# Ninth harmonic's products in 64-row matmuls, and feature rows doubled by ScalarE, in the fourth edge stage of a graph network

## The chip, the core and the metric

One core of one Trainium2 chip runs the whole network. The metric is device time in microseconds, the median of repeated runs.

## The reference, cut to what matters

Four graph layers follow each other on 3,125 nodes with 64 features and 53,125 edges sorted by destination. The change touches the fourth, an equivariant attention. With `x` the normalised features, per edge:

```
def tensor_product(x_e, sh, w, C):          # x_e [E,64], sh [E,9], C [64,9,128]
    acc = sh[:, 0:1] * (x_e @ C[:, 0, :])
    for s in range(1, 9):
        acc = acc + sh[:, s:s + 1] * (x_e @ C[:, s, :])
    return acc * w
k = tensor_product(x[edge_dst], edge_sh, wk, Cqk)     # keys,   128 columns
v = tensor_product(x[edge_dst], edge_sh, wv, Cv)      # values, 128 columns
attn = einsum('ehd,ehd->eh', q[edge_src], k)          # 8 heads of 16
alpha = segment_softmax(attn, edge_src)
upd = segment_sum(v * alpha, edge_src)                # then W_out, W_self, batch norm
```

(The reference hands `src, dst` over as this layer's `edge_dst, edge_src`, so the kernel gathers features by `src_i` and queries by `dst_i`.) The nine harmonics are a contraction over 9 x 64 = 576 rows: four and a half times the 128 rows of TensorE.

## The kernel before

Edges are padded to 416 tiles of 128, four tiles (GT = 4) to a **group**, so the stage has 104 groups. Weights of keys and values (`WKV`) were written to memory by the third stage. Each engine has its own instruction list; they meet at semaphores.

- **GpSimd (POOL)** gathers, per group, four tiles of feature rows from `XX` (L1780) into a ring `ga` of four groups, and four tiles of query rows from `QW` (L1770). `XX` has 128 columns: each node's 64 features, twice. The features are written twice by VectorE (L2035) and ScalarE (L1884) and stored before the stage (L1825).
- **SyncE (SP)** loads the harmonics, repeated over 64 partitions each: `shb` partitions 0 to 63 hold harmonics 0, 2, 4, 6, 8 (L1801), partitions 64 to 127 hold 1, 3, 5, 7 and zeros in the fifth place (L1802, L2039). It also loads `wkv` (L1794).
- **TensorE (PE)** in step s: `transposes(s)` puts the four doubled feature tiles, transposed, into bank 0 (L1926); `products(s-1, t)` for t = 0 to 3 are each five matmuls of 128 rows and 256 columns (L1935), which the profile shows as ten records, since an fp32 matmul has two passes; between them stand the sums over edges of group s-8 in two halves (L1916, L1917), and pieces of the softmax.
- **VectorE (DVE)** in step s: `harmonics(s)` multiplies bank 0 by `shb` into `z` (L2052), `keys_and_values(s-2)`, `add_sums(s-8)` in two halves (L2091, L2096), `values(s-7)` (L2079), and pieces of the softmax.
- **ScalarE (ACT)** in step s: one-hot matrices for group s-5 (L1845, L1849), and `weights(s-7)`: `ob` (L1856) and three copies into `D` (L1860), the latter behind a wait for `xb`, the split of the exponents that VectorE makes with its casts (L727 to L730).

The softmax works on four groups at once. Its pieces lie in two of every four steps: `soft_1` in steps with k % 4 == 2, `soft_2` in those with k % 4 == 3. In the second, VectorE ends the step with the exponents and their split (`split_steps`), then `values`. PE's list for a step begins

```
if lag(i, k, 0):
    transposes(i, k)
if p1:
    softmax_pe_0(pe, S3, q, 8, am3[:, b])
for t in range(GT):
    if kv:
        products(*kv, t)
    if old and t == 0:
        sums(*old, 0)
```

so whatever holds the transposes of group s holds the products of group s-1 too.

Of the kernel before, what the change touches and what calls it, by code (L numbers as in the profile page):

```python
# [27 lines left out]
ACT = mybir.ActivationFunctionType  # L28
AX = mybir.AxisListType

N = 3125
D = 64
E = 53125
PN = 125
# [58 lines left out]
def build(nc, A, out):  # L93
    with ExitStack() as ctx:
# [22 lines left out]
        def dram(name, shape, dt=F32):  # L117
            return nc.dram_tensor(name, shape, dt, kind="Internal").ap()
# [1463 lines left out]
        with nc.Block() as block:  # L1582
# [108 lines left out]
        w_self = sb("w_self", [D, D])  # L1691
        gcol = sb("gcol", [D, 1])
        bcol = sb("bcol", [D, 1])
        XX = dram("XX", [N, 2 * D])
        QW = dram("QW", [N, F])
        n3_l, n3_p, n3_dve, n3_var, n3_std, n3_t, n3_tc, n3_q, n3_qc, n3_ox, n3_oq, n3_h, n3_x = [sem("n3_" + x) for x in
            ("l", "p", "dve", "var", "std", "t", "tc", "q", "qc", "ox", "oq", "h", "x")]
        NL3 = 9
        R3 = rounds(NJ, 4)
        HALVES = [(slice(0, 12), 3), (slice(12, NJ), len(R3))]  # L1700
        PARTS = [(0, 3), (3, 5), (5, 7)]
# [3 lines left out]
        e3_g = [sem(f"e3_g{k}") for k in range(UG)]  # L1705
        QR = 4
        NODE3 = len(R3) * 5 + 2
        e3_zero = sem("e3_zero")
        e3_gq = [sem(f"e3_gq{k}") for k in range(UG)]
        e3_e = [sem(f"e3_e{k}") for k in range(2)]  # L1710
        e3_n = [sem(f"e3_n{k}") for k in range(2)]
# [15 lines left out]
        nodes = z[0:PN].rearrange("p a z e -> p (a z e)")  # L1727
        XC = nodes[:, 0:NJ * D].rearrange("p (j f) -> p j f", j=NJ)
        yn = nodes[:, NJ * D:2 * NJ * D].rearrange("p (j f) -> p j f", j=NJ)
        twice = nodes[:, NJ * D:3 * NJ * D].rearrange("p (j a f) -> p j a f", j=NJ, a=2)  # L1730
        D3 = tmp("D3", [128, 2, GT, 128], BF16)
        ob = tmp("ob3", [128, 2, GT * W], BF16)
        am3 = tmp("am3", [128, 2, 128])
# [29 lines left out]
        with nc.Block() as block:  # L1763
            @block.gpsimd
            def _(pool):
                def queries(g):
                    if g >= QR:
                        pool.wait_ge(e3_ev, (g - QR + 1) * 2)
                    for t in range(GT):
                        pool.indirect_dma_start(qg[:, (g % QR) * GT + t, :], None, QW, bass.IndirectOffsetOnAxis(  # L1770
                            ap=dst_i[:, g * GT + t:g * GT + t + 1], axis=0)).then_inc(e3_gq[g % UG], 16)

                pool.memset(ckv[D:128, NZ - 1, :], 0.0).then_inc(n3_p, 1)
                groups = NT // GT
                pool.wait_ge(n3_ox, len(HALVES) * 16)
                for g in range(groups):
                    if g >= GR:
                        pool.wait_ge(e3_X, g - GR + 1)
                    for t in range(GT):
                        pool.indirect_dma_start(ga[:, (g % GR) * GT + t, :], None, XX, bass.IndirectOffsetOnAxis(  # L1780
                            ap=src_i[:, g * GT + t:g * GT + t + 1], axis=0)).then_inc(e3_g[g % UG], 16)
                    if g == 1:
                        pool.wait_ge(n3_dve, NODE3)
                        pool.wait_ge(n3_oq, len(PARTS) * 16)
                    if g:
                        queries(g - 1)
                queries(groups - 1)

            @block.sync
            def _(sp):  # L1790
                def weights_load(i, k):
                    g = i * UG + k
                    wait(sp, e3_ev, (g - 1) * 2)
                    sp.dma_start(wkv[:, k % 2].rearrange("p t f -> p (t f)"),  # L1794
                                 WKV[:, bass.ds(g * GT * 2 * F, GT * 2 * F)]).then_inc(e3_n[k % 2], 16)

                def harmonics_load(i, k):
                    g = i * UG + k
                    cols = bass.ds(g * GT * W, GT * W)
                    wait(sp, e3_z, g - 1)  # L1800
                    sp.dma_start(shb[0:D, k % 2], A["ea9"][0:NS:2, cols].partition_broadcast(D)).then_inc(e3_e[k % 2], 16)  # L1801
                    sp.dma_start(shb[D:128, k % 2, 0:NZ - 1], A["ea9"][1:NS:2, cols].partition_broadcast(D)).then_inc(e3_e[k % 2], 16)  # L1802

                def body(i, k):
                    if lag(i, k, 0) and i * UG + k >= 2:
                        harmonics_load(i, k)
                    if lag(i, k, 2) and i * UG + k >= 4:
                        weights_load(*lag(i, k, 2))
                L = lambda o, i: sp.dma_start(o, i).then_inc(n3_l, 16)
                L(wq[:], A["L3_gnn_Wq"])  # L1810
                L(w_out[:], A["L3_gnn_W_out"])
                L(w_self[:], A["L3_gnn_W_self"])
                with nc.allow_non_contiguous_dma(reason="biases as columns"):
                    L(gcol[:], A["L3_gnn_gamma"].rearrange("a f -> f a"))
                    L(bcol[:], A["L3_gnn_beta"].rearrange("a f -> f a"))
                for m, w in ((ckv[:, :, 0:F], "Cqk"), (ckv[:, :, F:2 * F], "Cv")):
                    L(m[0:D, :, :], A["L3_gnn_" + w][:, 0:NS:2, :])
                    L(m[D:128, 0:NZ - 1, :], A["L3_gnn_" + w][:, 1:NS:2, :])
                for k in range(2):
                    harmonics_load(0, k)  # L1820
                for k in range(2):
                    weights_load(0, k)
                for h, (J, _) in enumerate(HALVES):
                    sp.wait_ge(n3_x, h + 1)
                    sp.dma_start(XX.rearrange("(p j) f -> p j f", p=PN)[:, J, :], twice[:, J].rearrange("p j a f -> p j (a f)")).then_inc(n3_ox, 16)  # L1825
                for part in PARTS:
                    sp.wait_ge(n3_qc, part[1])
                    sp.dma_start(QW.rearrange("(p j) f -> p j f", p=PN)[:, J_of(part), :], tab[:, J_of(part), :]).then_inc(n3_oq, 16)
                sp.wait_ge(e3_pad, 1)
                each_step(sp, body)  # L1830

            @block.scalar
            def _(act):
# [17 lines left out]
                def weights(i, k):  # L1851
# [7 lines left out]
                    for part in range(3):  # L1859
                        act.activation(D3[:, k % 2, :, part * 8:(part + 1) * 8],  # L1860
                                       exb[:, s, part, :].rearrange("p (x t) -> p t x", x=8)[:, kk * GT:(kk + 1) * GT, :],
                                       ACT.Copy).then_inc(e3_Mx, 1)

                def body(i, k):
                    p1, p2 = soft_1(i, k), soft_2(i, k)
                    if p1:
                        softmax_act_1(act, S3, p1[0] * 2 + p1[1], 8)
                    if p2:
                        softmax_act_3(act, S3, p2[0] * 2 + p2[1], 8)
                    if lag(i, k, 5):  # L1870
                        one_hots(*lag(i, k, 5))
                    if p2:
                        softmax_act_4(act, S3, p2[0] * 2 + p2[1], p2[1], 8, 1)
                        softmax_act_5(act, S3, p2[0] * 2 + p2[1], p2[1], fac_cols, 2)
                    if lag(i, k, SUMS - 1):
                        weights(*lag(i, k, SUMS - 1))
# [2 lines left out]
                    act.wait_ge(m2_x, r + 1)  # L1879
                    act.activation(yn[:, J, :], XC[:, J, :], ACT.Square).then_inc(m2_q, 1)  # L1880
                ln_std_step(act, n3_var, n3_std, 1)
                for h, (J, _) in enumerate(HALVES):
                    act.wait_ge(n3_h, h + 1)
                    act.activation(twice[:, J, 1, :], twice[:, J, 0, :], ACT.Copy).then_inc(n3_x, 1)  # L1884
                for r, (j0, n) in enumerate(R3):
                    act.wait_ge(n3_t, r + 1)
                    act.activation(HT[0:D, j0 * PN:(j0 + n) * PN], bank[r % 2][0:D, 0:n * PN], ACT.Copy).then_inc(n3_tc, 1)
# [7 lines left out]
            def _(pe):  # L1895
# [24 lines left out]

                def transposes(i, k):
                    g = i * UG + k
                    pe.wait_ge(e3_g[k], i * 64 + 64)
                    wait(pe, e3_z, g)
                    for t in range(GT):
                        last = pe.transpose(bank[0][:, t * 128:(t + 1) * 128], ga[:, (k % GR) * GT + t, :], ident[:])  # L1926
                    last.then_inc(e3_X, 1)

                def products(i, k, t):
                    g = i * UG + k  # L1930
                    if t == 0:
                        pe.wait_ge(e3_z, g + 1)
                        wait(pe, e3_ev, (g - 1) * 2)
                    for j in range(NZ):
                        last = pe.matmul(kv_of(k)[:, t, :], z[:, k % 2, j, t * 128:(t + 1) * 128], ckv[:, j, :],  # L1935
                                         start=(j == 0), stop=(j == NZ - 1))
                    if t == GT - 1:
                        last.then_inc(e3_V, 1)

# [29 lines left out]
                def node_transposes(r):  # L1969
# [2 lines left out]
                    if r >= 2:  # L1972
                        pe.wait_ge(n3_tc, r - 1)
                    for j in range(n):
                        last = pe.transpose(bank[r % 2][0:D, j * PN:(j + 1) * PN], twice[:, j0 + j, 0, :], ident[0:PN, 0:PN])
                    last.then_inc(n3_t, 1)

                def node_queries(r):
# [20 lines left out]
                        node_queries(r - 1)  # L1999
                node_queries(len(R3) - 1)  # L2000
                pe.wait_ge(n3_qc, len(R3))
                pe.wait_ge(n3_p, 1)
                pe.sem_inc(e3_S, SPARE)
                each_step(pe, body)

# [1 line left out]
            def _(dve):  # L2007
# [24 lines left out]
                dve.wait_ge(n3_std, 1)  # L2032
                c.link(dve.reciprocal(st[:, 5, :], st[:, 4, :]))
                for J, _ in HALVES:
                    dve.scalar_tensor_tensor(twice[:, J, 0, :], XC[:, J, :], 0.0, st[:, 5, J].unsqueeze(2).to_broadcast([PN, J.stop - J.start, D]),  # L2035
                                             ALU.max, ALU.mult).then_inc(n3_h, 1)
                c.mark(dve.tensor_scalar(dst_i[:], dst_i[:], 0, None, ALU.max))
                assert c.n == NODE3
                dve.memset(shb[D:128, :, NZ - 1, :], 0.0).then_inc(e3_pad, 1)  # L2039
                dve.memset(acc[:, 0:2, :], 0.0).then_inc(e3_zero, 1)  # L2040
                dve.memset(D3[:], 0.0).then_inc(e3_i, 1)
                dve.memset(crow[:], -BIG).then_inc(e3_i, 1)
# [4 lines left out]
                def harmonics(i, k):  # L2047
                    g = i * UG + k
                    dve.wait_ge(e3_X, g + 1)
                    dve.wait_ge(e3_e[k % 2], i * (UG // 2 * 32) + (k // 2 + 1) * 32)  # L2050
                    wait(dve, e3_V, g - 1)
                    dve.tensor_tensor(z[:, k % 2], bank[0][:].unsqueeze(1).to_broadcast([128, NZ, GT * W]), shb[:, k % 2],  # L2052
                                      ALU.mult).then_inc(e3_z, 1)
# [268 lines left out]
```

## Time and profile before

| | |
|---|---|
| median of 3 runs | 3109.23 us (3104.41 to 3112.86) |
| profiled execution: its time, its span | 3103.95 us, 3102.2 us |
| mean granted TensorE clock | 0.871 |
| first and last `harmonics` of the fourth stage | 1892.0 and 3001.3 us |
| busy in the span | PE 79%, DVE 71%, POOL 66%, ACT 28% |

A row of windows gives the stretch and its length, then busy us and number of instructions for PE, PE's weight loads, DVE, ACT and POOL, then the granted clock, the share of the DMA engines and GB/s. The profile is one execution. Times in a timeline are us from the start of the span. A granted clock of 1.00 is 2.4 GHz and 0.50 is 1.2 GHz. Busy time of PE counts overlapping records once; the end of a matmul is modelled, so the distance between starts says more than a duration.

### The profile page before, as it was taken

The numbers are of one execution on the slowest core, as the hardware profiler recorded it, in microseconds if no ns is written. First come the engines' busy times: TensorE is split into PE (matmuls) and PEld (weight loads), VectorE is DVE, ScalarE is ACT, GpSimd is POOL, SyncE is SP. The second block draws the span as 40 slices with busy tenths as digits, with TensorE's granted clock in tenths as the row PEclk, the third lists the DMA queues.
The fourth block names the chain that finished last, engine by engine and source line by source line (L and its number), as shares of the span: only waits on it lengthen the run. The fifth ranks groups of instructions, "written<-read, shape, count | busy, mean of one in ns | idle before, by whom it ended". The sixth has DMA issues, their size and how long they took to land. (4 is left out here: it accounts for less than half of the span.)

```text
span 3102.2 us, 51526 instructions
## 1 busy us (share of the span) xinstructions
PE 2460.4 (79%) x14042; PEld 2123.0 (68%) x14042; DVE 2187.5 (71%) x5057; ACT 868.7 (28%) x2421; POOL 2033.7 (66%) x2116
## 2 busy tenths in 40 slices
PE   5877777525766667477787767999999999999997
PEld 4777777424666666355565556888888888888884
DVE  4655555526888888555555564788888888888885
ACT  1111111136666664111111111223222233222233
POOL 4777777457777771177777745777777776767730
PEclk9777777657888888599989987999999999999996
DMA  3443333133333330044545456988889888898850
GB/s 85 94 93 87 86 86 85 31 65 65 59 60 61 61 56 7 29 153 153 162 153 161 153 150 162 219 213 206 206 206 213 208 206 203 209 211 208 202 137 11
DMA packets 333728, 404.37 MB, mean 130 GB/s; under 512 B 171120, under 2 KB 202974, under 8 KB 333538
## 3 DMA queue, kind: packets, MB, share of 16 engines
q1 hardware_dynamic: 252002, 251.19, 34.8%
q0 software_dynamic: 66560, 96.41, 14.0%
q10 hardware_dynamic: 14976, 54.53, 5.1%
q8 instruction: 84, 1.38, 0.2%
q14 instruction: 106, 0.87, 0.1%
HBM read 339.81 MB, written 62.07 MB: 130 GB/s over the span
## 5 line engine op out<-in xcount | busy, mean ns | idle before, releaser
L1935 PE MATMUL psum<-ckv,z 128*128 128x256 f32 x4160 | 968.2, 383 | 0.0
L1935 PEld LDWEIGHTS psum<-ckv,z 128*128 128x128 f32 x4160 | 766.9, 191 | 98.0
L1770 POOL DMA_INDIRECT acc<-QW,dst_i x416 | 400.2, 962 | 183.6 <-issue 111.2
L234 POOL DMA_INDIRECT ga<-TA,src_i x416 | 409.5, 984 | 160.8 <-issue 126.5
L1780 POOL DMA_INDIRECT ga<-XX,src_i x416 | 400.5, 963 | 163.8 <-issue 122.3
L1027 POOL DMA_INDIRECT ga<-T,src_i x416 | 402.5, 968 | 152.7 <-issue 125.9
L234 POOL DMA_INDIRECT ga<-T,src_i x416 | 399.2, 960 | 149.3 <-issue 124.3
L2052 DVE TENSOR_TENSOR z<-psum,shb 128x2560 f32<-128x2560 f32 x104 | 293.2, 2820 | 67.8 <-PE psum L1926 67.5
L1121 PE MATMUL psum<-HT,wy 128*128 128x128 f32 x1664 | 260.2, 320 | 69.0 <-DVE wy L1394 68.8
L445 PE MATMUL psum<-wre,re 128*128 128x68 f32 x832 | 208.6, 342 | 132.7 <-DVE oneT L290 80.9
L1121 PEld LDWEIGHTS psum<-HT,wy 128*128 128x128 f32 x1664 | 238.3, 228 | 87.1 <-DVE wy L1394 80.9
L445 PEld LDWEIGHTS psum<-wre,re 128*128 128x128 f32 x832 | 168.0, 250 | 154.8 <-issue 149.0
L1668 DVE TENSOR_TENSOR acc<-acc,psum 64x128 f32 x416 | 118.5, 285 | 158.3 <-PE psum L1623 114.0
L1623 PE MATMUL psum<-one,ga 128*128 128x128 f32 x832 | 129.1, 303 | 121.1 <-DMA ga<-T,src_i 109.4
L1623 PEld LDWEIGHTS psum<-one,ga 128*128 128x128 f32 x832 | 113.0, 208 | 152.7 <-issue 136.8
L1607 PEld LDWEIGHTS psum<-w2kv,hid 128*128 128x128 f32 x832 | 163.2, 196 | 72.0 <-issue 54.0
L446 PE MATMUL psum<-win,oneT 128*128 128x64 f32 x832 | 203.2, 335 | 0.0
L1607 PE MATMUL psum<-w2kv,hid 128*128 128x256 f32 x832 | 201.4, 386 | 0.0
L2096 DVE TENSOR_TENSOR acc<-acc,psum 128x256 f32 x416 | 175.5, 422 | 35.4 <-PE psum L1917 22.1
L1636 ACT ACTIVATE hid<-psum,b1kv 128x512 f32<-128x512 f32 x104 | 71.5, 687 | 455.1 <-PE psum L1615 455.1
L1202 DVE TENSOR_TENSOR acc<-acc,psum 128x256 f32 x416 | 173.4, 417 | 26.2 <-DVE acc L1202 8.6
L407 ACT ACTIVATE msg<-pre 128x256 f32<-128x256 f32 x104 | 43.5, 418 | 475.3 <-DVE pre L500 431.4
(366 smaller groups left out, 4198.2 us busy)
## 6 DMA issues: line engine op xcount, KB each, us to landing
shb<-in_ea SPq DMA_DIRECT2D x104, 640.0 KB
WKV<-wkvo ACTq DMA_DIRECT2D x104, 512.0 KB
shb<-in_ea SPq DMA_DIRECT2D x104, 512.0 KB
wkv<-WKV SPq DMA_DIRECT2D x104, 512.0 KB
dl<-DL SPq DMA_DIRECT2D x208, 128.0 KB
win<-TB SPq DMA_DIRECT2D x416, 32.0 KB
ga<-T,src_i POOLq DMA_INDIRECT x832
ef<-in_ea SPq DMA_DIRECT2D x104, 128.0 KB
```

The source lines that it names most:

```text
L234: pool.indirect_dma_start(o, None, table, bass.IndirectOffsetOnAxis(ap=src_i[:, g * GT + t:g * GT + t + 1], axis=0)).then_inc(s_g[k], 16)
L445: pe.matmul(P[:, o:o + D + 4], re[:, k % ER, t * W:(t + 1) * W], wre[:], start=True, stop=False)
L446: last = pe.matmul(P[:, o:o + D], oneT[:, k % 2, t * 128:(t + 1) * 128], win[:, k * GT + t, 0:D], start=False, stop=True)
L1027: pool.indirect_dma_start(ga[:, ring(g) + t, :], None, T1, bass.IndirectOffsetOnAxis(ap=src_i[:, g * GT + t:g * GT + t + 1], axis=0)).then ...
L1121: last = pe.matmul(sums_of(n)[:, a * 128:(a + 1) * 128], wy[:, g % YR, t, 2 * a:2 * a + 2, :].rearrange("p h f -> p (h f)"), one[:, g % OR ...
L1607: last = pe.matmul(kvp(k)[:, t * 256:(t + 1) * 256], hid[:, k % 2, t * 128:(t + 1) * 128], w2kv[:], start=True, stop=True)
L1623: last = pe.matmul(bank[k % 2][:, t * 128:(t + 1) * 128], ga[:, pair:pair + 2, :].rearrange("p a f -> p (a f)"), one[:, k * GT + t, :], st ...
L1770: pool.indirect_dma_start(qg[:, (g % QR) * GT + t, :], None, QW, bass.IndirectOffsetOnAxis(ap=dst_i[:, g * GT + t:g * GT + t + 1], axis=0) ...
L1780: pool.indirect_dma_start(ga[:, (g % GR) * GT + t, :], None, XX, bass.IndirectOffsetOnAxis(ap=src_i[:, g * GT + t:g * GT + t + 1], axis=0) ...
L1935: last = pe.matmul(kv_of(k)[:, t, :], z[:, k % 2, j, t * 128:(t + 1) * 128], ckv[:, j, :], start=(j == 0), stop=(j == NZ - 1))
L2052: dve.tensor_tensor(z[:, k % 2], bank[0][:].unsqueeze(1).to_broadcast([128, NZ, GT * W]), shb[:, k % 2], ALU.mult).then_inc(e3_z, 1)
L2096: dve.tensor_tensor(a, a, sums_of(half)[:, (t % 2) * 256:(t % 2 + 1) * 256].rearrange("p (r n) -> p r n", r=2), ALU.add).then_inc(e3_acc, 1)
```

## The change

- The ninth harmonic's fifth chunk, before a 128-row matmul per tile with 64 rows of zeros, becomes a 64-row matmul per tile. Tiles 0 and 1 use partitions 0 to 63, tiles 2 and 3 partitions 64 to 127, so `shb` and `ckv` hold the ninth harmonic and its weights there also. All four are issued ahead of tile 0's other matmuls, in the order 0, 2, 1, 3: the halves alternate, and so do the two banks of PSUM they write.
- `XX` holds each node once (64 columns). The gather fills columns 0 to 63 of `ga`; ScalarE copies them to columns 64 to 127 (`second_halves`), first in its step, after a wait for the gather. TensorE's transposes wait for that copy. The double features before the stage and their copy by ScalarE go.
- A third harmonics load per group for SP (64 partitions x 256 columns), two more weight loads.

```diff
-        XX = dram("XX", [N, 2 * D])
+        XX = dram("XX", [N, D])
...
-                pool.memset(ckv[D:128, NZ - 1, :], 0.0).then_inc(n3_p, 1)
...
-                        pool.indirect_dma_start(ga[:, (g % GR) * GT + t, :], None, XX, bass.IndirectOffsetOnAxis(
+                        pool.indirect_dma_start(ga[:, (g % GR) * GT + t, 0:D], None, XX, bass.IndirectOffsetOnAxis(
...
+                    late = bass.ds(g * GT * W + 2 * W, 2 * W)
+                    sp.dma_start(shb[D:128, k % 2, NZ - 1:NZ, 2 * W:], A["ea9"][NS - 1:NS, late].partition_broadcast(D)).then_inc(e3_e[k % 2], 16)
...
+                    L(m[D:128, NZ - 1:NZ, :], A["L3_gnn_" + w][:, NS - 1:NS, :])
...
-                    sp.wait_ge(n3_x, h + 1)
-                    sp.dma_start(XX.rearrange("(p j) f -> p j f", p=PN)[:, J, :], twice[:, J].rearrange("p j a f -> p j (a f)")).then_inc(n3_ox, 16)
+                    sp.wait_ge(n3_h, h + 1)
+                    sp.dma_start(XX.rearrange("(p j) f -> p j f", p=PN)[:, J, :], H[:, J, :]).then_inc(n3_ox, 16)
...
+                def second_halves(i, k):
+                    act.wait_ge(e3_g[k], i * 64 + 64)
+                    rows = ga[:, (k % GR) * GT:(k % GR + 1) * GT, :]
+                    act.activation(rows[:, :, D:F], rows[:, :, 0:D], ACT.Copy).then_inc(e3_two, 1)
+
                 def body(i, k):
                     p1, p2 = soft_1(i, k), soft_2(i, k)
+                    if lag(i, k, 0):
+                        second_halves(i, k)
...
-                for h, (J, _) in enumerate(HALVES):
-                    act.wait_ge(n3_h, h + 1)
-                    act.activation(twice[:, J, 1, :], twice[:, J, 0, :], ACT.Copy).then_inc(n3_x, 1)
...
-                    pe.wait_ge(e3_g[k], i * 64 + 64)
+                    pe.wait_ge(e3_two, g + 1)
...
                     if t == 0:
                         pe.wait_ge(e3_z, g + 1)
                         wait(pe, e3_ev, (g - 1) * 2)
-                    for j in range(NZ):
+                        for u in (0, 2, 1, 3):
+                            half = slice(0, D) if u < 2 else slice(D, 128)
+                            pe.matmul(kv_of(k)[:, u, :], z[half, k % 2, NZ - 1, u * 128:(u + 1) * 128], ckv[half, NZ - 1, :],
+                                      start=(u % 2 == 0), stop=False, skip_group_check=True)
+                    for j in range(NZ - 1):
                         last = pe.matmul(kv_of(k)[:, t, :], z[:, k % 2, j, t * 128:(t + 1) * 128], ckv[:, j, :],
-                                         start=(j == 0), stop=(j == NZ - 1))
+                                         start=False, stop=(j == NZ - 2), skip_group_check=True)
...
-                dve.memset(shb[D:128, :, NZ - 1, :], 0.0).then_inc(e3_pad, 1)
+                dve.memset(shb[D:128, :, NZ - 1, 0:2 * W], 0.0).then_inc(e3_pad, 1)
```

The rest of the diff renames `twice` to `H` where it is read and written, and adjusts counts of semaphores.

## Rows read from the trace of the kernel before

**Rows 1.** One window of 900 us in the fourth stage
```profile
2000.00:2900.00 900.00, 894.39 (x4846) 785.86 (x4845) 787.23 (x1605) 262.30 (x830) 652.23 (x679) 1.00 0.88 208
```
**Rows 2.** Groups of instructions by line, 2000 to 2900 us
```profile
L1935 PE MATMUL psum<-ckv,z 128*128 128x256 f32 x3329 | 773.4, 382 | 0.0
L1780 POOL DMA_INDIRECT ga<-XX,src_i x340 | 327.2, 962 | 103.7 <-issue 100.0 <-PE psum L1926 3.7
```
**Rows 3.** Waits, 2000 to 3000 us: total, times, longest
```profile
DVE acc L2096 <- PE psum L1917: 15.8, 23, 0.7
...
DVE z L2052 <- PE psum L1926: 11.4, 23, 0.6
```
**Rows 4.** Timeline, all engines: end of a soft_2 step and the step behind
```profile
2405.19 0.52 PE L701 MATMUL psum<-fdiag,sel 128*128 128x16 f32 x4
...
2405.55 0.63 PE L1926 MATMUL psum<-ident,ga 128*128 128x128 f32 x4
...
2407.34 0.23 DVE L730 CAST exb<-exf 128x128 bf16<-128x128 f32 x1
2407.66 0.56 ACT L1860 ACTIVATE D<-exb 128x32 bf16<-128x32 bf16 x3 [1.20 <-DVEq L732]
...
2408.12 1.26 ACT L1845 ACTIVATE one<-iota_row,dloc 128x128 f32<-128x128 f32 x4
2408.39 2.82 DVE L2052 TENSOR_TENSOR z<-psum,shb 128x2560 f32<-128x2560 f32 x1
...
2416.44 0.60 PE L1926 MATMUL psum<-ident,ga 128*128 128x128 f32 x4
...
2417.14 2.82 DVE L2052 TENSOR_TENSOR z<-psum,shb 128x2560 f32<-128x2560 f32 x1
```
**Rows 5.** Timeline of the next two steps
```profile
2424.89 0.42 DVE L2096 TENSOR_TENSOR acc<-acc,psum 128x256 f32 x1 [0.72 <-PE psum L1917]
...
2426.84 0.60 PE L1926 MATMUL psum<-ident,ga 128*128 128x128 f32 x4
...
2427.48 2.83 DVE L2052 TENSOR_TENSOR z<-psum,shb 128x2560 f32<-128x2560 f32 x1 [0.47 <-PE psum L1926]
...
2438.61 2.82 DVE L2052 TENSOR_TENSOR z<-psum,shb 128x2560 f32<-128x2560 f32 x1
```
**Rows 6.** Timeline of VectorE where the cycle of four closes
```profile
2451.59 2.82 DVE L2052 TENSOR_TENSOR z<-psum,shb 128x2560 f32<-128x2560 f32 x1
```
**Rows 7.** Groups by line and form, ScalarE, whole span
```profile
L407 ACT ACTIVATE msg<-pre 128x256 f32<-128x256 f32 x104 | 43.5, 418 | 475.3 <-DVE pre L500 431.4 <-PE psum L432 25.7 <-issue 18.2
```
**Rows 8.** Timeline near the stage's start
```profile
1911.68 1.12 PE L1926 MATMUL psum<-ident,ga 128*128 128x128 f32 x4 [4.66 <-DMA ga<-XX,src_i]
...
1912.59 11.33 PE L1935 MATMUL psum<-ckv,z 128*128 128x256 f32 x40
...
1924.19 8.80 PE L1935 MATMUL psum<-ckv,z 128*128 128x256 f32 x40
```
**Rows 9.** Windows in the same stretch, columns as in rows 1
```profile
1913.00:1917.00 4.00, 4.00 (x11) 3.17 (x10) 3.90 (x4) 0.00 (x0) 3.13 (x3) 0.50 0.17 49
1917.00:1919.00 2.00, 2.00 (x9) 1.68 (x8) 1.25 (x3) 0.00 (x0) 1.39 (x3) 0.82 0.77 212
```
**Rows 10.** Windows in the third stage, around pauses of PE
```profile
1704.50:1707.50 3.00, 0.41 (x3) 0.07 (x1) 1.91 (x3) 0.00 (x0) 2.10 (x3) 1.00 0.65 202
...
1744.50:1747.50 3.00, 0.44 (x3) 0.04 (x2) 1.83 (x3) 0.00 (x0) 2.11 (x3) 0.92 0.69 219
1747.50:1750.50 3.00, 3.00 (x10) 2.48 (x11) 0.55 (x2) 0.00 (x0) 2.39 (x3) 0.51 0.15 33
```
**Rows 11.** Timeline ahead of the stage
```profile
1864.52 1.25 SPq L1825 DMA_DIRECT2D XX<-z  x2
...
1878.65 0.95 POOL L1780 DMA_INDIRECT ga<-XX,src_i  x1 [37.25 <-DMA XX<-z]
```
**Rows 12.** Timeline of the stage's first gathers of queries
```profile
1894.51 0.94 POOL L1770 DMA_INDIRECT acc<-QW,dst_i  x1 [6.14 <-DMA QW<-vw]
```

More of the change, by code:

```diff
@@ L1697, in build @@
             ("l", "p", "dve", "var", "std", "t", "tc", "q", "qc", "ox", "oq", "h", "x")]
-        NL3 = 9
+        NL3 = 11
         R3 = rounds(NJ, 4)
@@ L1707, in build @@
         NODE3 = len(R3) * 5 + 2
-        e3_zero = sem("e3_zero")
+        e3_zero, e3_two = sem("e3_zero"), sem("e3_two")
         e3_gq = [sem(f"e3_gq{k}") for k in range(UG)]
@@ L1729, in build @@
         yn = nodes[:, NJ * D:2 * NJ * D].rearrange("p (j f) -> p j f", j=NJ)
-        twice = nodes[:, NJ * D:3 * NJ * D].rearrange("p (j a f) -> p j a f", j=NJ, a=2)
         D3 = tmp("D3", [128, 2, GT, 128], BF16)
@@ L1974, in node_transposes @@
                     for j in range(n):
-                        last = pe.transpose(bank[r % 2][0:D, j * PN:(j + 1) * PN], twice[:, j0 + j, 0, :], ident[0:PN, 0:PN])
+                        last = pe.transpose(bank[r % 2][0:D, j * PN:(j + 1) * PN], H[:, j0 + j, :], ident[0:PN, 0:PN])
                     last.then_inc(n3_t, 1)
@@ L2001, in _ @@
                 pe.wait_ge(n3_qc, len(R3))
-                pe.wait_ge(n3_p, 1)
                 pe.sem_inc(e3_S, SPARE)
@@ L2034, in _ @@
                 for J, _ in HALVES:
-                    dve.scalar_tensor_tensor(twice[:, J, 0, :], XC[:, J, :], 0.0, st[:, 5, J].unsqueeze(2).to_broadcast([PN, J.stop - J.start, D]),
+                    dve.scalar_tensor_tensor(H[:, J, :], XC[:, J, :], 0.0, st[:, 5, J].unsqueeze(2).to_broadcast([PN, J.stop - J.start, D]),
                                              ALU.max, ALU.mult).then_inc(n3_h, 1)
@@ L2049, in harmonics @@
                     dve.wait_ge(e3_X, g + 1)
-                    dve.wait_ge(e3_e[k % 2], i * (UG // 2 * 32) + (k // 2 + 1) * 32)
+                    dve.wait_ge(e3_e[k % 2], i * (UG // 2 * 48) + (k // 2 + 1) * 48)
                     wait(dve, e3_V, g - 1)
```

## The prediction, as put on record before the result

> **What bounds the kernel now.** I read the busy shares by window first, to find the stage's limit; then the groups by line, for what one group of edges costs each engine; then the waits, for who is really held; and then the timeline of four steps, because the softmax comes once in four groups and a mean over them hides where the slack lies.
>
> From 2000 to 2900 us PE is busy 894.39 of 900 us at clock 1.00, DVE 787 [rows 1]. The products alone are 3329 records, 83.2 groups of 40, and 773 us of the 894 [rows 1, 2]. So a group takes 900 / 83.2 = 10.81 us. POOL needs 0.962 us for a gather and 0.30 behind it (100.0 / 340 [rows 2]); I take the query gathers as the same. Eight of them are 10.1 us a group: POOL is 0.7 us from being the bound.
>
> DVE's 87% looks like slack, but the waits say otherwise: over 1000 us it waits for PE only 15.8 + 11.4 = 27 us [rows 3], 0.29 us a group. The rest of its idle time is its own waits from one instruction to the next. A PE of no cost would leave about 10.5 us a group. The four steps show the same. From one z to the next the distances are 8.75, 10.34, 11.13 and 12.98 us, together 43.20 [rows 4 to 6]. Only the second holds waits for PE, 0.72 and 0.47 us [rows 5]. PE's list for a plain step is 10.40 us (2416.44 to 2426.84 [rows 4, 5]).
>
> **The change, part by part.**
>
> *Products.* At 1924.19 forty passes take 8.80 us from the start of the first to the end of the last [rows 8]; one record is 0.382 us [rows 2]. So the pitch is (8.80 - 0.38) / 39 = 0.216 us, and the tail of a pass 0.17 us. Per group eight passes of 128 rows (1.73 us) go and eight of 64 rows come. No row shows 64-row matmuls on alternating halves, so I bound them. Perfectly paired they take four slots, 0.86 us: a saving of 0.87. Not overlapping at all, with the array run empty where the shape changes (twice 0.17), they take 2.07: a loss of 0.34. Between: passes start in order and each matmul has two on the same half (A A B B C C D D), so only the second of one and the first of the next overlap: five slots, 1.08 us, and one to two tails. I take 1.33 us, a saving of 0.40 us a group, so a plain PE step is 10.00 us.
>
> The tail of 0.17 us is what an emptied array would cost by the rows [rows 2, 8]. The Trainium skill's page "TensorEngine Tiling (Array Packing)", section "Key Properties", speaks against this change: a change of tiling mode drains TensorE, and there are two per group. By that rule the block takes 1.08 + 0.34 = 1.42 us and the step 10.09; with no drain 1.08 and 9.75. The cycle worked out below would lose 2.14 or 1.46 us by these, instead of 1.96.
>
> *The copy on ScalarE.* 128 x 256 elements take 0.418 us [rows 7]; ScalarE is busy 262 of 900 us [rows 1], so its time costs nothing. Its place does. It stands first in step s+1 of ScalarE's list, behind `weights(s-7)` of step s, and in a soft_2 step those end with the `D` copies, which wait for DVE's last cast. That cast ends at 2407.34 + 0.23 = 2407.57; the `D` copies start at 2407.66 and the next ScalarE instruction could start at 2408.12 [rows 4]. The copy then ends near 2408.54. Before, PE began these transposes at 2405.55 [rows 4], right behind the softmax's small matmuls of 2405.19. In the changed kernel PE waits about 3 us there, and behind the waiting transposes in its list stand the products of the group before, whose z has long been ready, and the sums, for which DVE waits.
>
> Where does it go? DVE's z comes at: last cast 2407.57, + 0.97 (copy done), + 0.06 release and 0.2 weight load, + 0.60 transposes, + 0.04 = 1.87 us behind the cast, against 0.82 before (2408.39 [rows 4]). So the fourth distance grows by 1.05 to 14.03. Then PE has had no lead left: transposes directly ahead of z, and a whole PE step between two transposes. So the first distance is no longer DVE's 8.75 but PE's 10.00, and the second too is 10.00 (before 10.34; DVE's own is 9.15). The third stays DVE's 11.13. Sum 10.00 + 10.00 + 11.13 + 14.03 = 45.16 us, 1.96 more than 43.20. There are 26 softmax blocks, and 24 of their soft_2 steps have transposes behind them: 24 x 1.96 = **+47 us**.
>
> *The clock.* PE's small matmuls wait for DVE, so they stay near 2405.19 + 0.52 in that frame (at most 0.8 us earlier), and the transposes move to about 2408.8. PE is idle 3 to 4 us, with little work just ahead. In this trace a pause of 4.66 us was followed by clock 0.50 up to about 1917.6, the transposes taking 1.12 instead of 0.60 and 40 passes 11.33 instead of 8.80 [rows 8, 9]: 3.0 us of PE's time. In the third stage pauses near 2.6 us come about every 10 us; the clock mostly stays at 1.00, as at 1704.5, but in about one of four falls to 0.50, as at 1744.5, for some 3 us of work [rows 10], which costs 1.5 us. The new pause lies between, nearer to the long one. I take a fall in 21 of 24 and 2.2 us each: 21 x 2.2 = **+46 us**. It falls on the two steps where PE has become the bound, so it isn't hidden. The page "TensorE: Matmul & The Clock Gate" of the Trainium skill, section "Loop structure matters more than you think", warns of the same: matmuls behind a long wait run cold. The rows agree at 4.66 us and are mixed at 2.6.
>
> *Gather and loads.* The feature gather moves half the bytes, the third harmonics load adds 64 KB against 128 KB less, on DMA engines busy 0.88 [rows 1]; SP issues one more DMA of about 0.6 us a group and has room. The loads for a group are asked for two steps ahead, about 18 us. Cost 0; if the cover were gone, a DMA a fraction of a microsecond late per group. POOL's 10.1 us stay below the new 11.3.
>
> *Ahead of the stage.* `XX` has half the bytes and is stored without ScalarE's copy. POOL now starts at 1878.65, 13 us behind the two stores' issue of 1864.52 [rows 11]; half of that may go. But its second round waits for the query table until 1894.51 [rows 12], so most is only an earlier wait. I take -2 us, bounds -6 and +1. The first seven groups run at POOL's rate; nothing comes of PE's saving there. The tail behind the last z doesn't change.
>
> Sum: 47 + 46 - 2 = +91 us. The profiled execution took 3103.95 us (span 3102.2), which would become 3195; the runs' median is 5.3 us above it, so 3109.23 + 91 = **3200 us**.
>
> **The rivals.**
>
> *The stall without the clock.* If PE's pause leaves the clock at 1.00, as most pauses of 2.6 us do [rows 10], only 47 - 2 remain: 3154. With perfect pairs the PE step is 9.54 and the cycle 44.24 (+1.04): 25 us, and -6 ahead: 3128, the low bound.
>
> *Pairs that don't overlap.* The PE step is 10.73, the cycle 10.73 + 10.73 + 11.13 + 14.03 = 46.62 (+3.42): 82 + 46 - 2 = 126, so 3235. With 3.0 us for each of 24 falls it is 82 + 72: 3263, the high bound. For it speaks that two passes of a matmul share a half, against it that the halves and banks alternate.
>
> *Faster: the copy is hidden everywhere.* If ScalarE had the doubled rows ready before PE came, the 0.72 + 0.47 us in the second distance would vanish and the other three stay: 42.01 us, -1.19 x 24 = -29, with -2 ahead 3078. It decides by one thing: whether the copy ends ahead of 2405.55 in the frame of [rows 4]. It is queued behind the `D` copies of 2407.66. Only if PE's lead in that step were not needed at all would the result come near this.
>
> *No change.* The stall costs less than worked out (PE's lead partly kept) and the clock stays, so that about 1 us a cycle of loss meets the saving of rival three.
>
> **How the numbers follow.** Within 0.3%, 9 us, no difference can be told. Chances: forecast with stall and clock (3165 to 3230) 0.58; stall without clock (3128 to 3165) 0.18; no overlap (3225 to 3263) 0.12; hidden copy 0.07; no change 0.05. Slower 0.88, same 0.05, faster 0.07. The range is 3138 to 3240: it leaves out the faster and unchanged cases (0.12) and the ends of the second and third (about 0.07).
>
> **What the changed profile would show.** In every fourth step the wait of PE's transposes for ScalarE's copy, 3 to 4 us, directly behind `D`; z 1.9 us behind the last cast; clock 0.50 for 3 to 6 us in 21 of 24 such places; distances near 10 + 10 + 11.1 + 14, with 2 us more on the first. The eight 64-row passes within about 1.3 us. PE's busy share falls from 99% though DVE's falls too. The prediction is wrong if PE does not wait for the copy there, if DVE's z in the step behind comes at 8.75 again, if the clock reads 1.00 throughout, or if the 64-row block takes over 1.8 us.

## The result, and the profile after

The changed kernel takes 3204.45 us (median of 4 runs, 3201.53 to 3207.88) against 3106.82 us before: a ratio of 1.032, with a 95% interval from 1.0302 to 1.0337. The prediction was 3200 us, in a range from 3138 to 3240. The profiled execution has a span of 3199.8 us, 97.6 more than before.

One window of the fourth stage, columns as in [rows 1]:

```profile
2000.00:2900.00 900.00, 827.56 (x4391) 682.33 (x4390) 718.58 (x1449) 261.32 (x831) 585.10 (x614) 0.93 0.78 183
```

Every engine is less busy than in [rows 1], and the clock is 0.93 in the mean. No engine has become a bound. Waits have come, and the waits from 2000 to 3000 us (total, times, longest) name them:

```profile
PEld psum L1931 <- ACT ga L1868: 78.0, 21, 4.2
...
DVE acc L2104 <- PE psum L1922: 74.8, 59, 2.6
...
DVE z L2060 <- PE psum L1931: 38.5, 63, 1.3
```

The first row is new: 21 times in 1000 us PE waits for the copy. The other two are those of [rows 3], 27 us then and 113 us now: VectorE waits for a TensorE that has come late. The timeline at the end of one soft_2 step answers to [rows 4]:

```profile
2440.69 0.59 PE L701 MATMUL psum<-fdiag,sel 128*128 128x16 f32 x4
...
2443.61 0.23 DVE L730 CAST exb<-exf 128x128 bf16<-128x128 f32 x1
2443.92 0.56 ACT L1861 ACTIVATE D<-exb 128x32 bf16<-128x32 bf16 x3 [1.89 <-DVEq L732]
...
2444.39 0.40 ACT L1868 ACTIVATE ga<-ga 128x256 f32<-128x256 f32 x1
...
2444.84 1.12 PE L1931 MATMUL psum<-ident,ga 128*128 128x128 f32 x4 [3.56 <-ACT ga L1868]
...
2445.99 2.83 DVE L2060 TENSOR_TENSOR z<-psum,shb 128x2560 f32<-128x2560 f32 x1 [1.25 <-PE psum L1931]
```

This is the chain that the prediction named: last cast, `D` copies, the new copy, transposes, z. The transposes take 1.12 us instead of 0.63, so z comes 2.15 us behind the cast (2443.84 to 2445.99), where 1.87 was worked out at full clock and 0.82 was seen before. Windows of the same place show the clock:

```profile
2443.00:2444.50 1.50, 0.00 (x0) 0.00 (x0) 1.20 (x4) 0.58 (x4) 1.08 (x2) 0.62 1.09 391
2444.50:2446.00 1.50, 1.16 (x6) 0.84 (x6) 0.25 (x2) 1.47 (x6) 1.00 (x2) 0.50 0.16 34
2446.00:2449.00 3.00, 3.00 (x11) 1.99 (x12) 3.00 (x2) 1.99 (x6) 1.82 (x2) 0.50 0.16 31
...
2450.50:2452.00 1.50, 1.50 (x12) 1.37 (x11) 1.24 (x4) 0.00 (x0) 0.94 (x1) 1.00 0.77 208
```

The clock falls inside the pause and is back at 1.00 some 5 us behind the restart. It fell at each of the 22 pauses from 2000 to 3050 us (3.55 to 4.07 us long); the mean time at half clock behind a restart was about 5.2 us. The one pause of the stage at which it did not fall lasted 2.48 us.

The 64-row block, by the weight loads of PE in one plain step:

```profile
2504.87 0.57 PEld L1931 LDWEIGHTS psum<-ident,ga 128*128 128x128 f32 x4
2505.61 0.73 PEld L1941 LDWEIGHTS psum<-ckv,z 64*128 64x128 f32 x8 [0.17 <-issue]
2506.68 1.59 PEld L1944 LDWEIGHTS psum<-ckv,z 128*128 128x128 f32 x8 [0.33 <-issue]
```

From the first 64-row load to the next 128-row load are 1.07 us, and the engine's loads stand idle ahead of each change of shape (0.17 and 0.33 us). In the kernel before no load waits at this place. I read this as the array running empty twice; how much time it costs is measured in p11_in_place below. A plain step of PE is 9.94 us (transposes at 2409.66 and 2419.60), where 10.00 was forecast.

Read from the starts of z in the timelines, medians over the stage, in us (the first distance follows the soft_2 step; the last column is the mean cycle of four steps from group 8 to group 96):

| kernel | 1st | 2nd | 3rd | 4th | mean cycle |
|---|---|---|---|---|---|
| before | 8.75 | 10.33 | 11.13 | 12.98 | 43.40 |
| changed | 12.00 | 10.11 | 11.29 | 14.30 | 47.67 |

### The profile page after: what moved, and what is told of

The parts are those of the page before. It is cut to its first block and busy times, and to the rows that moved or that the text cites. A ratio compares the mean times of both kernels' runs of the same rounds, so it can differ in the third digit from the quotient of the medians.

```text
span 3199.8 us, 51733 instructions
## 1 busy us (share of the span) xinstructions
PE 2485.4 (78%) x14042; PEld 2086.3 (65%) x14042; DVE 2194.6 (69%) x5057; ACT 900.0 (28%) x2523; POOL 2022.1 (63%) x2115
## 5 line engine op out<-in xcount | busy, mean ns | idle before, releaser
L1944 PE MATMUL psum<-ckv,z 128*128 128x256 f32 x3328 | 822.0, 395 | 0.0
L1944 PEld LDWEIGHTS psum<-ckv,z 128*128 128x128 f32 x3328 | 625.2, 196 | 125.2 <-issue 42.8
L1769 POOL DMA_INDIRECT acc<-QW,dst_i x416 | 393.6, 946 | 298.8 <-DVE vw L2075 190.0
L1846 ACT ACTIVATE one<-iota_row,dloc 128x128 f32<-128x128 f32 x416 | 131.8, 388 | 185.4 <-PE psum L1922 185.4
```

## The experiments

All medians below are set against the kernel before on the same chip (3103.6 to 3106.3 us).

**p1_products.** The change's products without its copy: the kernel before with

```diff
+  third harmonics load, ninth harmonic's weights also on partitions 64 to 127
+  for u in (0, 2, 1, 3): 64-row matmuls ahead of tile 0's others
   (XX and the gathers stay 128 columns wide, no second_halves)
```

> The 64-row products alone: features gathered double as before, no copy on ScalarE. Theory (the copy's place is the whole loss, the new products are a gain): PE's plain step 9.94 us as in the changed kernel, VectorE becomes the bound, the four distances of z are about 8.75, 9.15, 11.1, 13.0 (sum 42.0 against 43.2), no fall of the clock after the softmax step, time 3078 (24 x -1.2 us), ratio near 0.991. Rival (the change of matmul shape costs as much as it saves): distances as before, 3100 to 3112. Rival (the 64-row block itself is a loss): over 3120.

3098.67 us (3087 to 3127 in ten runs), ratio 0.9991 (0.9964 to 1.0018): no difference to the kernel before can be told. The medians of the distances are near the theory's: 8.75, 9.34, 11.35, 12.92. But the mean cycle is 43.34, because some second and third steps are longer, up to 13.4 us, and the time is not 3078. Waits and one window say why:

```profile
DVE z L2057 <- DMA shb<-in_ea: 16.8, 17, 2.6
```

```profile
2000.00:2900.00 900.00, 870.23 (x4878) 721.35 (x4876) 788.68 (x1610) 262.16 (x830) 654.95 (x679) 1.00 1.00 214
```

The DMA engines are busy all the time, and z waits for the harmonics. I read this as a third load together with double gathers being more than they carry at this pace; p8_no_third_load takes the load away, and p7_early_mid further down has the load with single gathers (DMA share 0.94, 3084.75 us). So the halved gather is not there for nothing, a thing that neither of my theories had.

**p8_no_third_load.** The same without the third load. The kernel leaves out the ninth harmonic's part of tiles 2 and 3, which it multiplies by zeros, so it serves only to measure time:

```diff
-  sp.dma_start(shb[D:128, k % 2, NZ - 1:NZ, 2 * W:], ...)
+  dve.memset(shb[D:128, :, NZ - 1, :], 0.0)     # whole row zero, as before
```

> The kernel with the 64-row products alone and double gathers, without the third harmonics load: the ninth harmonic of tiles 2 and 3 is left out (multiplied by zeros). Theory (that kernel's VectorE waited for harmonics on DMA engines busy all the time): DMA share down from 1.00 to about 0.95, no wait of z for shb, 3080 to 3090 against 3099. Rival (the waits come from something else): 3099.

3084.22 us, ratio 0.9936 (0.9920 to 0.9951). DMA share 0.92, no wait of z for `shb`, mean cycle 42.39:

```profile
2000.00:2900.00 900.00, 879.59 (x4953) 733.03 (x4952) 803.62 (x1638) 265.26 (x840) 674.87 (x693) 1.00 0.92 213
```

So the third load on top of the double gathers costs p1_products some 15 us.

**p2_copy.** The change's copy without its products:

```diff
-  for u in (0, 2, 1, 3): ...   # 64-row matmuls
-  for j in range(NZ - 1): ...
+  for j in range(NZ): ...      # five 128-row matmuls per tile, two loads, as before
```

> The copy on ScalarE alone, products all in 128-row matmuls as before. Theory: the same wait of the transposes in every fourth step and the same fall of the clock, with a PE step of 10.4 us in place of 9.94, so the two steps bound by PE cost 0.9 us more in a cycle of four than in the changed kernel: 3204 + 24 x 0.9 = 3226. Rival (the stall comes from the products' new form or from loads): near 3110.

3196.62 us, ratio 1.0295 (1.0274 to 1.0316). That the stall is the copy's is shown: the kernel loses 90 us with no 64-row matmul in it. The size was missed by 30 us, and the other way: it is faster than the whole change. Its distances are 12.08, 10.40, 11.13, 13.85. The second is PE's longer step, as expected; the first should have been near 13. PE, which comes later to the transposes, pauses less:

```profile
2443.30 0.93 PE L1929 MATMUL psum<-ident,ga 128*128 128x128 f32 x4 [2.87 <-ACT ga L1866]
```

2.87 us, not 3.56. The clock falls at 20 of 23 such pauses and is then at 0.50 for 3.4 us, nearly all of it behind the restart; in the changed kernel it is at 0.50 for about 6.6 us a pause, 5.2 of them behind the restart (windows of half a microsecond added up from 1970 to 3070 us). Because it falls later, the transposes here still take 0.93 us and not 1.12. The kernel also holds its own comparison: in the cycles without a fall the first distance is 10.40 us instead of mostly 12.1, the fourth is somewhat longer, and the cycle is 46.0 to 46.7 us against mostly 47.4. By an estimate from these figures, 25 to 30 of the 90 us lost are the clock's, where p4_warm below finds 57 of 98 in the changed kernel. So a faster PE waits longer for the same cast and gets the clock back later, and in the changed kernel this is enough to eat the products' whole gain. No run of this kernel with a filled pause was made, so that last step is an estimate.

**p4_warm.** The changed kernel with PE kept at work during the pause:

```diff
+  wait(pe, e3_z, g)
+  if k % KG == 0 and g >= 2 * KG:
+      for _ in range(7):
+          pe.matmul(bank[0][:, 0:2 * F], ident[:], ckv[:, 0, :], start=True, stop=True)
   pe.wait_ge(e3_two, g + 1)
-  wait(pe, e3_z, g)
```

(The wait for VectorE's reading of bank 0 had to go ahead of the extra matmuls, which write there; the transposes still wait for the copy in all 22 places from 2000 to 3000 us, 20.1 us in total, so the extra work does not itself hold them.)

> The changed kernel with seven extra fp32 matmuls of 128 x 256 into bank 0 ahead of the wait for the copy, in the step behind each second softmax step (24 places); their result is overwritten by the transposes. PE is busy for 3.0 of the 3.6 us that it would wait. Theory (the clock's fall is a term of its own, 5.1 us at half clock behind each pause, 2.6 us of PE's time): granted clock 1.00 there, time 3204 - 24 x 2.6 = 3142. Rival (the clock's fall is hidden behind VectorE): 3195 to 3205.

3152.34 us, ratio 1.0144 (1.0127 to 1.0161), 10 us above the expected number. The clock is 1.00 from 2000 to 2900 us:

```profile
2000.00:2900.00 900.00, 885.17 (x4912) 738.64 (x4911) 759.73 (x1531) 276.96 (x878) 619.33 (x650) 1.00 0.84 193
```

The distances are 9.94, 10.19, 11.29, 13.85, the mean cycle 45.31: 2.36 us less than in the changed kernel, 57 us over 24 cycles (52 in the medians of time; the profiled start of the stage was 7 us later here). This splits the loss into its two parts: stall 45.31 - 43.40 = 1.91 us a cycle, clock 2.36. The clock's part lies in the first distance (12.00 against 9.94) and in the fourth (14.30 against 13.85), which ends behind transposes at half clock.

**p3_early.** The changed kernel with the copy for the next group, first in the step:

```diff
-  if lag(i, k, 0):
-      second_halves(i, k)
+  if i == 0 and k == 0:
+      second_halves(0, 0)
+  if i * UG + k + 1 < NT // GT:
+      second_halves(*((i, k + 1) if k + 1 < UG else (i + 1, 0)))
```

> The changed kernel with the copy for the next group issued one step earlier, first in ScalarE's step. Theory (the loss is where the copy stands, not what it costs): no wait of the transposes for the copy, clock 1.00 in the stage, VectorE the bound as in the run with the products alone, 3070 to 3080. Rival (ScalarE's extra 0.4 us per group or its wait for the gather delays the softmax): 3090 or more.

3089.42 us, ratio 0.9945 (0.9928 to 0.9962): 115 us less than the changed kernel by moving one instruction in ScalarE's list. The distances are 8.75, 9.34, 11.13, 12.91. It misses the 3070 to 3080 in part by two steps near the start, one of them of 15.15 us:

```profile
2003.43 0.42 ACT L1868 ACTIVATE ga<-ga 128x256 f32<-128x256 f32 x1 [6.11 <-DMA ga<-XX,src_i]
...
2003.76 0.26 ACT L706 ACTIVATE dT<-psum 128x128 f32<-128x128 f32 x1
...
2004.05 0.29 DVE L635 TENSOR_TENSOR pen<-dT 128x127 f32<-128x127 f32 x1 [3.93 <-ACT dT L706]
```

While the gathers are barely ahead, the early copy waits for one, and the softmax's ScalarE instruction waits behind it. The start of the stage is later too: the eighth z comes at 1968.08 us, 5.7 later than in the kernel before.

**p7_early_mid.** The copy one group ahead, placed behind `softmax_act_1` and `softmax_act_3` instead of ahead of them.

> The changed kernel with the copy one group ahead, but placed behind the softmax's first ScalarE instruction of the step instead of ahead of it. In the run with the copy first in the step, two steps near the stage's start lost 4 and 2 us because ScalarE waited for the next gather ahead of the softmax. Theory: those go, 3083 to 3087. Rival (noise or another cause): 3089 or more.

3084.75 us (five runs), ratio 0.9933 (0.9919 to 0.9946). This version beats both kernels, by 21 us and by 120. The softmax's waits behind the copy are gone, and the eighth z comes at 1962.36 us as before. Its mean cycle is 42.46. In 1000 us z waits for PE and for loads only 2.4 us in all, so VectorE's own list sets the pace; the window of 2000 to 2900 us has clock 1.00:

```profile
2000.00:2900.00 900.00, 879.45 (x4952) 732.74 (x4951) 801.75 (x1639) 295.32 (x934) 669.12 (x691) 1.00 0.94 206
```

**p6_early_copy_only.** p2_copy with the copy one group ahead, first in the step (128-row products).

> Copy one step ahead, with the products all in 128-row matmuls: the half of the change that the run with the early copy had beside the 64-row products. Theory (a hidden copy costs nothing and saves nothing; the gain of the early copy's run is the 64-row products'): as the kernel before, 3100 to 3108. Rival (the halved gather is what gains): 3090.

3112.90 us, ratio 1.0026 (1.0017 to 1.0035), 5 us above the expected band. The distances are those of before, 8.75, 10.33, 11.13, 12.98. A hidden copy and a halved gather give nothing here and cost about 0.2%. Part of the cause stands in the trace of the one profiled execution (3106.61 us, the fastest of the ten). It has the same wait as p3_early, near the stage's start:

```profile
1956.97 0.42 ACT L1866 ACTIVATE ga<-ga 128x256 f32<-128x256 f32 x1 [10.99 <-DMA ga<-XX,src_i]
...
1957.58 0.29 DVE L635 TENSOR_TENSOR pen<-dT 128x127 f32<-128x127 f32 x1 [7.32 <-ACT dT L706]
```

Its eighth z is 4.0 us later than before, and from there the cycle is as before (43.37 against 43.40). That the slower runs, which were not profiled, lose more at the same place is not shown. The DMA share is 0.84 instead of 0.88.

**p5_order.** The changed kernel with `for u in range(GT)` for `for u in (0, 2, 1, 3)`.

> The changed kernel with the four 64-row matmuls in the order 0, 1, 2, 3: two of the lower half, then two of the upper, in place of 0, 2, 1, 3. Theory (passes overlap only across halves, eight passes in four slots of 0.216 us when they alternate): only one pair of neighbours lies on different halves, about seven slots, the block 0.5 to 0.65 us longer, which two PE-bound steps of four feel: 3204 + 24 x 1.1 = 3230. Rival (order is of no matter): 3204.

3209.40 us, ratio 1.0338 (1.0322 to 1.0354), all four distances as in the changed kernel (12.02, 10.11, 11.28, 14.30). The theory fell. The block in the timeline of PE:

```profile
2511.07 1.14 PE L1941 MATMUL psum<-ckv,z 64*128 64x256 f32 x8
2512.14 1.99 PE L1944 MATMUL psum<-ckv,z 128*128 128x256 f32 x8
```

1.07 us again. I formed another: that a 64-row pass is short by itself, whatever its neighbours' half.

**p9_lower_half.** The kernel before, with the four 64-row matmuls all on partitions 0 to 63 and nothing else changed:

```diff
-  half = slice(0, D) if u < 2 else slice(D, 128)
+  half = slice(0, D)
   (no third load, double gathers, no copy)
```

> The kernel before with only this: the ninth harmonic's four products as 64-row matmuls ahead of tile 0's others, all on partitions 0 to 63; features gathered double, no copy, no third harmonics load. Theory (as the run with the order 0, 1, 2, 3 suggests, a 64-row pass takes 0.107 us whichever half the one before it was on): the eight passes within about 1.13 us, distances of z 8.75, 9.34, 11.13, 13.1, DMA share near 0.92, 3080 to 3087. Rival (passes overlap only because other matmuls lie on the other half): block 1.8 us or more, 3106 to 3120.

3134.59 us, ratio 1.0101 (1.0084 to 1.0117), above the rival's band as well. That theory fell too:

```profile
2507.89 1.99 PE L1935 MATMUL psum<-ckv,z 64*128 64x256 f32 x8
2509.81 1.99 PE L1938 MATMUL psum<-ckv,z 128*128 128x256 f32 x8
```

The block is 1.92 us, longer than the 1.73 of the eight 128-row passes, and PE's plain step is 10.79 us instead of 10.40. PE then sets the pace in part: the distances are 9.17, 10.92, 11.61 and 12.92, the mean cycle 44.75, 1.35 more than before, which is 32 us over 24 cycles. So overlap needs work on both halves, and within four matmuls it made no difference in which of the two orders they were given. The banks alternate here as in the changed kernel, so it is not they that bring the overlap.

**p10_lower_early.** p9_lower_half with single gathers and the copy placed as in p7_early_mid.

> As the run with all four 64-row matmuls on the lower half, with single gathers and the copy one group ahead behind the softmax's first ScalarE instruction. VectorE is the bound in both, so the halved gather can only help where DMA or the first gathers held it: theory 3078 to 3086, the same as the kernel without the copy within 5 us. Rival (the halved gather is needed): at least 10 us faster than the kernel without the copy.

3133.75 us, ratio 1.0098 (1.0082 to 1.0115), the same as p9_lower_half. The time it was to have, 3078 to 3086, went with p9_lower_half's theory; that the halved gather is worth nothing without the third load stands, in this pair as in p6_early_copy_only.

**p11_in_place.** The kernel before, each tile's last matmul cut to 64 rows where it stands:

```diff
   for j in range(NZ):
-      last = pe.matmul(kv_of(k)[:, t, :], z[:, k % 2, j, t * 128:(t + 1) * 128], ckv[:, j, :], ...)
+      rows = slice(0, D) if j == NZ - 1 else slice(0, 128)
+      last = pe.matmul(kv_of(k)[:, t, :], z[rows, k % 2, j, t * 128:(t + 1) * 128], ckv[rows, j, :], ...)
```

> The kernel before with the ninth harmonic's matmul of each tile cut to 64 rows where it stands, last of its tile: eight changes of shape per group in place of two. Theory (the array empties at each change of shape, about 0.2 us each by the block's 1.6 us from transposes to the next 128-row matmul less eight passes): PE's step 10.4 - 0.87 + 8 x 0.2 = 11.1 us, PE the bound nearly everywhere, cycle about 45.5 us, 3106 + 24 x 2.2 = 3159. Rival (a change of shape costs nothing, the block's extra comes once): 3080.

3238.28 us, ratio 1.0429 (1.0411 to 1.0446), 79 us more than expected. The distances are 11.44, 11.92, 12.29, 12.91.

```profile
2504.89 2.52 PE L1936 MATMUL psum<-ckv,z 128*128 128x256 f32 x10
2507.34 0.49 PE L1916 MATMUL psum<-one,edge_a 128*128 128x128 f32 x2
```

This tile takes 2.45 us from start to next start, against 2.16 before (10 x 0.216): 0.29 us. But part of the price falls on what stands behind it. PE's plain step, from transposes to transposes, is 11.90 us (2516.86 to 2528.76) against 10.40, with the same number of passes: 1.50 us more for four changes to 64 rows and back, 0.37 us each. The expected number had given each change 0.2 us, 0.4 there and back, which is near; but it had also given each lone 64-row pass 0.107 us, which p9_lower_half disproved. The step of 11.1 us was 0.8 us short, mostly by that.

## Why the prediction was right, step by step

**The stall.** Right in place, direction and size: 24 x 1.96 = 47 us forecast; 24 x 1.91 = 46 us in p4_warm, which has the stall without the clock. p3_early and p7_early_mid show that it is the copy's place and nothing else of it: there the same copy costs none of this.

**The step bound by PE.** The first and second distances were to be 10.0 each at full clock and are 9.94 and 10.19 in p4_warm, the third 11.13 and is 11.29, the fourth 14.03 and is 13.85. Each is off by up to 0.2 us, and the errors nearly cancel, so the sum is closer than its parts; why the third grew is not shown. DVE's own second distance, put at 9.15, is 9.34 in the runs where PE does not bind.

**The clock.** The right term, undersized: 46 us forecast (21 falls of 24 at 2.2 us each), 57 us by the cycles of p4_warm and the changed kernel. A fall came at nearly every pause (23 of 24) and cost 2.36 us a cycle; 5.2 us of half clock behind the restart would be up to 2.6 us of PE's work. The two rows between which I chose, 1.5 and 3.0 us, did hold it. I put all of it on the two steps bound by PE; it came in the first and fourth distances (2.06 and 0.45 us), none in the second. This was the term with the weakest support, and it is more than half of the loss.

**The 64-row products.** The saving of a PE step was forecast as 0.40 us and is 0.46. The reasoning was off in detail. I had assumed five slots in order, and one to two tails of 0.17 us for the emptying. The saving of 0.46 us means that the eight passes cost 1.73 - 0.46 = 1.27 us in all. With the 0.37 us that p11_in_place gives for a pair of changes, 0.90 us is left for the passes: close to four slots (0.86), not five. So one figure was too high and the other too low, and they nearly cancel, which is luck. The Trainium skill's page "TensorEngine Tiling (Array Packing)", section "Key Properties", says that a change of tiling mode drains TensorE. The 0.37 us agree with that. The rival without overlap (PE step 10.73) did not come here, but p9_lower_half is that case: block 1.92 us, PE step 10.79.

**Gather and loads.** Cost 0 in the changed kernel, as forecast (DMA share 0.78 at the slower pace, and no wait of z for a load from 2000 to 3000 us). At the faster pace of p1_products it is not 0: there the third load needs the halved gather. That coupling was missing from the prediction.

**Ahead of the stage.** -2 us forecast. The eighth z starts at 1959.43 instead of 1962.38, -3 us, and the tail behind the last z is 1.7 us shorter. The first z came 9.3 us earlier, and most of that was, as forecast, only an earlier wait. The sum: 46 + 57 - 3 - 1.7 = 98, measured 97.6. The forecast difference was 91; that 3200 lies within 5 us of 3204.45 is helped by its start from 3109.23, 2.4 us above the kernel before in the final comparison.

**The rivals.** Stall without clock: it would have been 3154, and p4_warm, made into that case, takes 3152. Hidden copy: worked out as 3078; p7_early_mid takes 3084.75, with a cycle of 42.46 instead of 42.01. No change: it needed a stall of about 1 us a cycle and no fall of the clock; both the stall (1.91) and the clock (2.36) are against it.

## What to carry to other kernels

Ask of an added instruction not what it costs but what it stands behind: 0.4 us on an engine busy 28% of the time cost 100 us, because in every fourth step it was queued behind a wait for the slowest chain, and the bound engine's list was queued behind it. A pause of TensorE has a second price in the clock, which can exceed the first. And read the list of the engine one step ahead: here the remedy was to issue the same copy one group earlier, behind the softmax's instructions, and the two halves of the change (half the gather, a third load) only pay together.

## What the runs showed of the hardware

- Four 64-row fp32 matmuls of 256 columns, two on each half of the rows, take 1.07 us up to the next 128-row load at granted clock 1.00, in the order 0, 2, 1, 3 as in 0, 1, 2, 3 (p5_order); all on one half they take 1.92 us, and four 128-row ones 1.73. I had expected order to matter.
- A change from 128 to 64 rows and back cost 0.37 us of PE's step in p11_in_place (11.90 against 10.40 us for four).
- The price of a pause was higher for the longer ones. Pauses of 2.79 to 3.38 us (median 2.87) left the clock at 0.50 for 3.4 us, or at 3 of 23 did not make it fall (p2_copy); pauses of 3.55 to 4.07 us (median 3.56) left it there for about 6.6 us (changed kernel), all but one of 3.63 us, behind which it was 3.4. Length alone does not decide: in p2_copy pauses of 2.79 us are found both with and without a fall.
- DMA engines at a share of 1.00 (p1_products) showed as scattered late loads and a wide spread of run times, 3087 to 3127 us, not as an even slowing. At 0.92 and 0.94 z waited for a load twice at most, 2.2 us in 1000 (p8_no_third_load, p7_early_mid).
